# One block for the softmax and the weighing of a graph attention layer, with shares by logarithm and scatters dealt out anew

## The reference

```python
kj = k[src] + e                                  # e = edge_attr @ We
vj = v[src] + e
alpha = jnp.einsum('ehc,ehc->eh', q[dst], kj) / np.sqrt(C)
amax = jax.ops.segment_max(alpha, dst, num_segments=n)
ex = jnp.exp(alpha - amax[dst])
denom = jax.ops.segment_sum(ex, dst, num_segments=n)
alpha = ex / (denom[dst] + 1e-16)                # the share of an edge
agg = jax.ops.segment_sum(vj * alpha[:, :, None], dst, num_segments=n)
out = agg.reshape(n, HID) + (x @ Wskip + bskip)
```

## Time and profile before

| | us |
|---|---|
| median of 3 runs | 5401.89 |
| lowest and highest run | 5398.77, 5412.19 |
| span of the profiled execution, from its first to its last instruction | 4651.0 |
| `softmax_maxima`, from 2061 to 2197 | 136.0 |
| `weigh_values`, from 2197 to 2400.7 | 203.7 |
| m1 and l2, from 2400.7 to 2568.6 | 167.9 |

### The profile page before, as it was taken

How to read it: one execution, slowest core, us unless ns; L and a number is a source line. 1 busy time by engine, 2 the same in 40 slices (tenths; PEclk the granted TensorE clock), 3 DMA queues, 4 the chain that set the end, 5 groups by cost and what they waited for, 6 DMA issues and landing times. The chain is left out here.

```text
span 4651.0 us, 50018 instructions
## 1 busy us (share of the span) xinstructions
PE 2871.3 (62%) x13750; PEld 2210.0 (48%) x13751; DVE 2230.8 (48%) x2711; ACT 613.9 (13%) x1076; POOL 3414.1 (73%) x3213
## 2 busy tenths in 40 slices
PE   3799998967777777751989643444444333333333
PEld 1688887943333333331989433333333333333333
DVE  7899997656666666668971621111111111111112
ACT  0355554010000000001751000000000000000000
POOL 1888886857777777767867677777777777777775
PEclk8899999968877878875999866666666566555556
DMA  6466566816666666651989523222222122212221
GB/s 191 139 189 183 170 187 209 265 37 172 170 170 170 170 171 173 173 153 59 278 241 276 174 68 94 68 68 68 68 68 68 49 53 52 53 53 53 53 53 51
DMA packets 498663, 599.91 MB, mean 129 GB/s; under 512 B 190115, under 2 KB 367441, under 8 KB 496248
## 3 DMA queue, kind: packets, MB, share of 16 engines
q0 software_dynamic: 117856, 246.12, 19.4%
q1 hardware_dynamic: 337751, 229.77, 17.7%
q10 hardware_dynamic: 42944, 122.68, 7.3%
HBM read 406.69 MB, written 204.36 MB: 131 GB/s over the span
## 5 line engine op out<-in xcount | busy, mean ns | idle before, releaser
L1151 PE MATMUL ps<-got,g_hot 128*128 x3224 | 719.2, 414 | 1151.3 <-DMA got<-y_back,s_msg 597.5
L721 POOL DMA_INDIRECT rec_by_src<-rec,pos x782 | 1123.9, 1437 | 344.1 <-issue 245.8
L1151 PEld LDWEIGHTS ps<-got,g_hot 128*128 128x128 f32 x3224 | 667.8, 316 | 1213.1 <-issue 1213.1
L1612 POOL DMA_INDIRECT sc_kv<-kv,d_src x806 | 762.0, 945 | 254.9 <-issue 245.3
L1036 POOL DMA_INDIRECT got<-y_forward,d_msg x782 | 739.1, 945 | 238.2 <-issue 238.2
L1036 POOL DMA_INDIRECT got<-y_back,s_msg x766 | 722.7, 943 | 241.7 <-issue 233.1
L806 PE MATMUL ps<-ln_low,ln_hot 128*125 128x256 f32 x2848 | 618.9, 380 | 19.7 <-DVE ln_low L783 15.9
L806 PEld LDWEIGHTS ps<-ln_low,ln_hot 128*125 128x125 f32 x2848 | 535.3, 188 | 103.2 <-issue 22.7
L1059 DVE TENSOR_TENSOR g_hot<-ps,src_loc 128x1024 f32<-128x1024 f32 x101 | 123.4, 1224 | 832.1 <-PE ps L1151 831.7
L1715 PE MATMUL ps<-q,sc_hotT 128*128 x1616 | 274.2, 322 | 236.4 <-DVE sc_hotT L1657 207.4
L1067 DVE TENSOR_TENSOR g_y<-ps,ms_b 128x384 f32<-128x384 f32 x75 | 41.8, 558 | 732.1 <-PE ps L1164 732.1
(11 more groups left out here) (328 smaller groups left out, 3102.4 us busy)
## 6 DMA issues: line engine op xcount, KB each, us to landing
linked<-ln_out SPq DMA_DIRECT2D x320, 224.0 KB
ve<-sc_kve ACTq DMA_DIRECT2D x202, 256.0 KB
wv_ve<-ve SPq DMA_DIRECT2D x101, 512.0 KB, 5.0
l_links<-linked SPq DMA_DIRECT2D x25, 800.0 KB, 7.3
l_links<-linked ACTq DMA_DIRECT2D x25, 800.0 KB, 9.2
attr_pairs<-ln_feats POOLq DMA_DIRECT2D x7, 2048.0 KB
sc_attr<-attr_pairs SPq DMA_DIRECT2D x202, 64.0 KB, 2.6
sc_kv<-kv,d_src POOLq DMA_INDIRECT x806, 3.0
```

What stands on the lines that cost most here:

```text
L721: pool.indirect_dma_start(out=dram["rec_by_src"], out_offset=bass.IndirectOffsetOnAxis(ap=S["pos"][:, c:c + 1], axis=0), in_=S["rec"][:, c ...
L1151: last = pe.matmul(ps[:, bass.ds(columns[j], width)], hot[:, q, j, :], got[:, bass.ds(slots[j], width)], start=False, stop=True, skip_grou ...
L1612: pool.indirect_dma_start(out=kv[:, q, j, :], out_offset=None, in_=dram["kv"], in_offset=bass.IndirectOffsetOnAxis(ap=S["d_src"][:, c:c + ...
```

## The change

The two blocks become one, `softmax_and_weigh`. The node lists and places are loaded in `scores`, in SP's loop at step 24; the -1 is stored in `index_stage`. ACT's Exp writes to `mx_back` and leaves the scores; after the sums ACT takes the logarithm of each head's sums (with 1e-16 added as bias), DVE subtracts it from the scores, and ACT's Exp gives the shares. SP issues the first six loads of values ahead of the stores of the shares. ACT makes its masks of the first three groups, and DVE its masks of the same groups, before the shares are back. The clearing of PSUM is cut in two, 2048 columns early and 1152 behind the first weighing; the transposes back use three banks from the fifth on. At the start of each round of six groups DVE copies that round's shares (192 columns) into PSUM bank 7 (`hand`), and the multiplication reads them there. ACT's first step writes into `wv_hot` itself, not into a buffer of its own. `RECORD_PARTS` is dealt out anew; in `index_stage` ten records go ahead of the gathers. The diff, cut to its core (of `weigh_values`, whose lines move into the new function, only what changes is shown):

```diff
-RECORD_PARTS = {"index": 6, "link": 302, "l0": 70, "m0": 30, "project": 22, "maxima": 82, "weigh": 100, "m1": 42, "l2": 76, "norm": 0}
+RECORD_PARTS = {"index": 16, "link": 302, "l0": 70, "m0": 38, "project": 22, "maxima": 16, "weigh": 138, "m1": 42, "l2": 86, "norm": 0}
...
+            if send is not None:
+                first, last = part_of(send)
+                send_some(pool, S, dram, first, last - LATER)
             for k, s in enumerate(stairs):
...
-                send_records(pool, S, dram, send)
+                send_some(pool, S, dram, last - LATER, last)
...
+                if n == 4 * WAYS:
+                    for name, a in (("before", dram["node"][0:rows]), ("node", dram["node"][1:1 + rows]), ("after", dram["node"][2:2 + rows]),
+                                    ("place", dram["loc"].rearrange("b e -> (b e)")[0:rows])):
+                        sp.dma_start(S["mx_" + name][:, :], a.rearrange("(p c) -> p c", p=P)).then_inc(S["noded"], 16)
...
-def softmax_maxima(nc, S, dram):
+def softmax_and_weigh(nc, S, dram):
...
+        iota = ps[:, 7 * BANK:7 * BANK + P]
+        share = ps[:, 7 * BANK + P:7 * BANK + P + HEADS * WAYS * GROUP].rearrange("p (a c) -> p a c", a=HEADS)
...
+            pe.wait_ge(cleared, 2)
+
+            def group(i, q):
+                columns = load_columns(nc, S, mybir.EngineType.PE, "dst", 1, start_of(i, q))
+                pe.wait_ge(heated[q], i + 1)
+                pe.wait_ge(faced[q], i + 1)
+                pe.wait_ge(weighed[q], i + 1 + (q == WAYS - 1))
+                for j in range(GROUP):
+                    last = pe.matmul(ps[:, bass.ds(columns[j], D)], hot[:, q, j, :], ve[:, q, j, :],
+                                     start=False, stop=True, skip_group_check=True)
+                last.then_inc(summed[q], 1)
+
+            with pe.Fori(0, WHOLE) as i:
...
             send_records(pool, S, dram, "maxima")
+            send_records(pool, S, dram, "weigh")
...
-                act.activation(score[:, h, :], score[:, h, :], ACT.Exp).then_inc(exped, 1)
+                act.activation(back[:, h, :], score[:, h, :], ACT.Exp).then_inc(exped, 1)
+            for h in range(HEADS):
+                act.wait_ge(tallied, h + 1)
+                act.activation(back[:, h, :], back[:, h, :], ACT.Ln, bias=guard[:, 0:1]).then_inc(logged, 1)
+            for h in range(HEADS):
+                act.wait_ge(weighted, h + 1)
+                act.activation(score[:, h, :], score[:, h, :], ACT.Exp).then_inc(shared, 1)
+
+            def face(n):
+                i, q = divmod(n, WAYS)
+                act.wait_ge(summed[q], i + 1)
+                for j in range(OWN, GROUP):
+                    c = n * GROUP + j
+                    last = act.activation(hot[:, q, j, :], S["col"][:, :], ACT.Abs, bias=S["dst_loc"][:, c:c + 1], scale=-1.0)
+                last.then_inc(apart, 1)
+                act.wait_ge(apart, n + 1)
+                act.activation(hot[:, q, OWN:GROUP, :], hot[:, q, OWN:GROUP, :], ACT.Relu, bias=S["ones"][:, 0:1], scale=-1.0).then_inc(faced[q], 1)
+
+            for n in range(FIRST):
+                face(n)
...
+            for n in range(WAYS):
+                bring(n)
             for h in range(HEADS):
                 sp.wait_ge(shared, h + 1)
...
+            dve.wait_ge(S["noded"], 16 * 4)
...
-                link(dve.tensor_scalar_add(back[:, h, :], back[:, h, :], 1e-16))
-                link(dve.reciprocal(back[:, h, :], back[:, h, :]))
-                dve.tensor_tensor(score[:, h, :], score[:, h, :], back[:, h, :], ALU.mult).then_inc(shared, 1)
-            dve.wait_ge(shared, HEADS)
...
+                dve.engine_nop().then_inc(tallied, 1)
+            for h in range(HEADS):
+                dve.wait_ge(logged, h + 1)
+                dve.tensor_tensor(score[:, h, :], score[:, h, :], back[:, h, :], ALU.subtract).then_inc(weighted, 1)
+            dve.wait_ge(weighted, HEADS)
+            dve.wait_ge(turned, HR)
+            dve.wait_ge(kept, HR)
+            dve.memset(ps[:, 0:TURN_AT * BANK], 0.0).then_inc(cleared, 1)
             dve.tensor_copy(iota[:, :], S["col"][:, :]).then_inc(numbered, 1)
             dve.wait_ge(numbered, 1)
+            dve.sem_inc(weighed[WAYS - 1], 1)
+
+            def hand(i):
+                dve.wait_ge(weighed[WAYS - 1], i + 1)
+                dve.tensor_copy(share, S["alpha"][:, :, bass.ds(start_of(i, 0), WAYS * GROUP)]).then_inc(handed, 1)
+                dve.wait_ge(handed, i + 1)
+
+            def mark(i, q):
                 dve.wait_ge(summed[q], i + 1)
                 dve.tensor_tensor(hot[:, q, 0:OWN, :], iota[:, :].unsqueeze(1).to_broadcast([P, OWN, P]),
                                   S["dst_loc"][:, bass.ds(start_of(i, q), OWN)].unsqueeze(2).to_broadcast([P, OWN, P]), ALU.is_equal).then_inc(heated[q], 1)
+
+            def weigh(i, q):
                 dve.wait_ge(landed[q], (i + 1) * 16)
                 ve4 = ve[:, q].rearrange("p k (a c) -> p k a c", c=HEAD)
+                dve.tensor_tensor(ve4, ve4, share[:, :, q * GROUP:(q + 1) * GROUP].rearrange("p a k -> p k a")
                                   .unsqueeze(3).to_broadcast([P, GROUP, HEADS, HEAD]), ALU.mult).then_inc(weighed[q], 1)
 
+            for q in range(FIRST):
+                mark(0, q)
+            dve.wait_ge(done, HR)
+            hand(0)
+            weigh(0, 0)
+            dve.memset(ps[:, TURN_AT * BANK:BLOCKS * D], 0.0).then_inc(cleared, 1)
+            for q in range(1, WAYS):
+                if q >= FIRST:
+                    mark(0, q)
+                weigh(0, q)
+            with dve.Fori(1, WHOLE) as i:
+                hand(i)
                 for q in range(WAYS):
+                    mark(i, q)
+                    weigh(i, q)
+            hand(WHOLE)
             for q in range(REST):
+                mark(WHOLE, q)
+                weigh(WHOLE, q)
```

More of the change, by code:

```diff
@@ L471, in _ @@
             if send is not None:
-                send_records(pool, S, dram, send)
+                send_some(pool, S, dram, last - LATER, last)
         @block.sync
         def _(sp):
+            sp.wait_ge(fronted, 1)
+            sp.dma_start(dram["node"][0:1].rearrange("(a n) -> a n", a=1), front[:, :]).then_inc(begun, 16)
             for k, s in enumerate(stairs):
@@ L488, in _ @@
             sp.wait_ge(filed, 16 * len(stairs))
+            sp.wait_ge(begun, 16)
             if sent:
@@ L1744, in softmax_maxima @@
         turn = m.sb("mx_turn", [P, HR, P])
-        node = m.sb("mx_node", [P, L])
-        node_b = m.sb("mx_before", [P, L])
-        node_a = m.sb("mx_after", [P, L])
-        loc = m.sb("mx_loc", [P, L])
+        node, node_b, node_a, loc = (S["mx_" + name] for name in ("node", "before", "after", "place"))
         bad = m.sb("mx_bad", [P, L])
@@ L1752, in softmax_maxima @@
         back = m.sb("mx_back", [P, HEADS, L])
-        open_b, open_a, open_s = (m.sb("mx_open" + n, [P, L]) for n in ("before", "after", "same"))
+        open_b, open_a, open_s = node, m.sb("mx_openafter", [P, L]), loc
         ends = m.sb("mx_ends", [P, 2 * HEADS])
@@ L1789, in _ @@
                     pe.wait_ge(refilled[h], 16)
-                if n >= 4:
-                    pe.wait_ge(done, n - 3)
-                pe.transpose(ps[:, (n % 4) * BANK:(n % 4) * BANK + P], turn[:, n, :], S["ident"][:, :]).then_inc(turned, 1)
+                if n >= 3:
+                    pe.wait_ge(done, n - 2)
+                pe.transpose(turned_back(n), turn[:, n, :], S["ident"][:, :]).then_inc(turned, 1)
+            pe.wait_ge(cleared, 2)
[9 more added lines that the diff above has]
+            with pe.Fori(0, WHOLE) as i:
+                for q in range(WAYS):
+                    group(i, q)
+            for q in range(REST):
+                group(WHOLE, q)
         @block.gpsimd
@@ L1809, in _ @@
                 act.wait_ge(turned, HR + n + 1)
-                act.activation(S["alpha"][:, h, c * P:(c + 1) * P], ps[:, (n % 4) * BANK:(n % 4) * BANK + P], ACT.Copy).then_inc(done, 1)
+                act.activation(S["alpha"][:, h, c * P:(c + 1) * P], turned_back(n), ACT.Copy).then_inc(done, 1)
             act.wait_ge(done, HR)
+            for n in range(FIRST, GROUPS):
+                face(n)
+            for q in range(WAYS):
+                act.wait_ge(faced[q], WHOLE + (q < REST))
         @block.sync
         def _(sp):
-            sp.wait_ge(fronted, 1)
-            sp.dma_start(dram["node"][0:1].rearrange("(a n) -> a n", a=1), front[:, :]).then_inc(stored, 16)
-            sp.wait_ge(stored, 16)
-            for t, a in ((node_b, dram["node"][0:P * L]), (node, dram["node"][1:1 + P * L]),
-                         (node_a, dram["node"][2:2 + P * L]), (loc, flat_loc[0:P * L])):
-                sp.dma_start(t[:, :], a.rearrange("(p c) -> p c", p=P)).then_inc(noded, 16)
             for h in range(HEADS):
@@ L1834, in _ @@
                              dram["alpha"][h].rearrange("(c p) e -> p c e", p=P)).then_inc(refilled[h], 16)
```

(30 more changed lines are left out.)

90 lines of the change are left out of this document (31 added, 59 removed).

## The result

The changed kernel takes 5527.55 us (median of 4 runs, 5522.1 to 5537.37), the kernel before 5401.58: a ratio of 1.0224 with a 95% interval of 1.0206 to 1.0243. It is 126 us slower, where I had forecast 18 us less.

The account below looks back on a forecast made before the run. The softmax was taken as a serial chain on DVE, the weighing as bound by PE and DVE level. Terms -6.3 - 21.6 - 3.7 + 6.1 + 7.6 = -17.9 us gave 5384.0 us, range 5366 to 5403.

Parts of the forecast that it names:

- the 750.9 us: Whole kernel: difference between profiled span 4651.0 us and median 5401.89, kept unchanged in the forecast.
- The 154 records of the joint block: Softmax and weighing: 28 fewer records on POOL, which would be done earlier still; no effect on time.
- Start of the softmax: Block start to first work on the scores: early node lists and masks gain 6.3 us, at most 9.4.
- Division: First carry to last share: logarithm, subtraction and Exp replace reciprocal and multiplication, 31.85 to 10.25 us, gaining 21.6.
- Way back: Last share to first product of the weighing: 19.0 us becomes some 15.4, gaining 3.7, between 1 and 5.
- Loop: Weighing rounds: `hand` adds 0.68 us a round, less savings; 6.1 us lost in all, bounds 0 to +25.
- a dear copy: Rival, weighing loop: `hand` costs its upper bound, 1.84 us a round, giving 5402.6, no change; chance 0.10.
- values bound by DMA: Rival, weighing: early start only moves the wait, loop takes back half of 31.6 us, giving 5399.8; chance 0.05.
- the rival that had it twice as long: Rival, weighing: multiplication with repeated PSUM shares takes twice 1.22 us, costing 123 us, giving 5507; chance 0.08.
- The records in l2: Block of m1 and l2: ten more records make POOL end 7.6 us after PE, lengthening the block by 7.6.
- m0: Stage m0: eight more records, 10.2 us, fit in an idle of 15.12 us; no effect.
- `index_stage`: Ten records ahead of the first gather, 12.7 us within POOL's 18.43 us wait: nothing, at most 12.7.

Follow-up runs that it names:

- the run with slower records: Changed kernel with three small POOL clearings ahead of each of the 138 later records, no pause: 5415.03 us, ratio 1.0009 against the kernel before.
- the second profile of the kernel before: The kernel before, unchanged, profiled once more: 5398.07 us, span 5396.3.
- The pause with shares from SBUF: Changed kernel; POOL waits after 60 records for PE's first round, then sends 94; weighing reads shares from SBUF without copies: 5408.33 us, ratio 0.9992.

## Why the prediction was wrong

Two steps failed, and they have one root.

- "I keep the 750.9 us between them as they are." That difference was not a constant outside the stages. It lay in them: 263 us in `scores`, 139 in m1 with l2, 270 in the gathering sums, and so on, in stretches in which POOL issues one indirect transfer after another. A span a seventh below the timed median should have been taken as a sign that the traced execution lacked something that the timed ones have.
- "The 154 records of the joint block: [...] With 28 fewer it is done earlier still: nothing." Earlier is what cost the time. Before, POOL was through with its 82 records when the shares came back, stood still at the end of the block, and was then held to one record in 1.87 us by DVE's multiplications. Now nothing stops it at the way back, DVE has nothing to multiply there, records go out at 1.27, PE crawls, so DVE goes on waiting, so records go on at 1.27: the state keeps itself up until the records are out. (Reading the shares from SBUF doesn't end it, 418.5 us, as there is no multiplication to lengthen a record while DVE waits.) The crawl costs 109.5 us by the run with slower records (423.8 against 314.3); less the 23.4 that the rest of the change gains in this block, that is the 86 us. I had looked at POOL only as an engine that may end a block, not as one that slows another. POOL's pause and its first slow records in the second profile of the kernel before:

```profile
2489.90 0.97 POOL L721 DMA_INDIRECT rec_by_src<-rec,pos  x1 [8.53 <-POOLq L1742]
...
2496.68 1.56 POOL L721 DMA_INDIRECT rec_by_src<-rec,pos  x1 [0.31 <-issue]
2498.55 1.56 POOL L721 DMA_INDIRECT rec_by_src<-rec,pos  x1 [0.30 <-issue]
```

The rest, by the terms, where the crawl is kept away (the run with slower records, block 314.3 us; the forecast's sum gives 337.7 - 25.5 = 312.2):

- Start of the softmax: right. 18.1 us to the scores (18.4 in the changed kernel), forecast 18; 6 us gained.
- Division: right, 9.97 us against 10.25. The logarithm takes 1.07 us for 816 columns with its neighbour's overlap (four in 4.30), four subtractions take 3.78 and four Exp 3.20, a little less than assumed. Exp's table load starts 0.02 us behind the last logarithm and Exp 0.01 behind the load; the pause that the Trainium skill, "ScalarE: Activation LUTs", section "What ACT_TABLE_LOAD costs", adds to a switch of tables doesn't show here either, its 1283 ns does (1.28).
- Way back: too hopeful. From last share to first product it is 18.6 us in that run and not 15.4: 0.4 us gained on the earlier trace rows, not 3.7, and nothing on the second profile of the kernel before, which has 17.9 (2477.93 to 2495.78).
- Loop: right. A round takes 11.89 us where 11.88 were forecast, the copy 0.36; the block with the copies is 5.0 us longer than the one without (314.3 against 309.3), the term was 6.1. So the rivals of a dear copy and of values bound by DMA fall. The multiplication from PSUM takes 1209 ns, which disposes of the rival that had it twice as long:

```profile
L2011 DVE TENSOR_TENSOR wv_ve<-wv_ve,ps 128x1024 f32<-128x1024 f32 x101 | 122.1, 1209 | 8.8 <-DMA wv_ve<-ve 8.7
```

- The records in l2: right that they cost, wrong why. Not POOL's end but the crawl counts there, and each of the ten costs its 1.3 us from the first: 13.2 us, not 7.6. The same in m0, where I had put nothing: some 11 us.
- `index_stage`: right, nothing.

With the terms as measured, block -23.4 by that run (314.3 against 337.7), l2 +13.2 and m0 +11, the sum is +0.8 us: without the crawl in the joint block the change would have come out even. The run with slower records agrees (1.0009). The pause with shares from SBUF, whose block is 5 us shorter without the copies, gives 0.9992.

Open: what PE and a dense row of indirect transfers share. That the pace of the records brings the crawl on is shown by the runs above; how it does so is not. The crawl's waits have no releaser in the profile, and ACT and SP show such pauses too (in l2 of the kernel before ACT stood 96.5 us ahead of a copy whose input had been there for some 80 us); whether it is the fetching of instructions, or the writing of something, the trace's own records included, wasn't tried. Some of it can be narrowed from the trace of the changed kernel: from 2541 to 2611, in the crawl, the queues that carry instructions moved a single packet (8 KB at 2567.76, in 1.55 us), so that a wait for such a packet can't stand ahead of each product; the DMA engines are busy for 0.08 of their time there and for 0.86 in the loop (rows below), so that it isn't their load; and the lower clock adds 0.25 us to a product, not the 1.7 to 3.1 us of waiting ahead of it. Why the first trace of the kernel before is free of the crawl isn't known either: the runs that list a span have it 1.7 to 1.9 us below their time, but that trace has no time of its own. So a dense row of records is not enough by itself in every execution. Nor was it tried whether the gathers of `scores` and of the sums could be spaced with profit.

## What to carry to other kernels

When a profile's span and the timed median differ by more than the ends of the program can hold, take a second profile before using its durations. An engine that is off the path can still slow the one on it: look at what happens to PE's rate in each stretch where POOL issues indirect transfers back to back, and count a transfer there at its full time. Spacing them, with a cheap instruction that takes some 0.4 us, can make the whole faster.

## What the runs showed of the hardware

- While POOL issued indirect scatters of 0.97 us every 1.27 to 1.30 us, PE started 0 to 8 products in nearly every ten microseconds of the timed executions (the joint block of the changed kernel, m1 with l2 of the kernel before); at one in 1.42 us 5 to 11 in most; at 1.65, 1.82 and 1.87 its full 84 to 90. The zeros stand in m1, where PE's next product needs a copy that ACT started 96.5 us late: ACT is held up as well. PE returned to its rate some 10 us after the last record. The first trace of the kernel before, whose span lies so far below the timed runs, has records at 1.27 us in l2 and no crawl.
- In the crawl PE's clock falls as well. Two stretches of the changed kernel, in the crawl and in the loop at full rate, columns as above:

```profile
2550.00:2610.00 60.00, 7.81 (x22) 6.04 (x21) 2.87 (x3) 3.20 (x8) 43.54 (x46) 0.50 0.08 18
2650.00:2800.00 150.00, 144.69 (x1230) 141.96 (x1229) 146.75 (x166) 122.36 (x306) 0.00 (x0) 1.00 0.86 268
```

  The granted clock is 0.50, the lower of its two levels (1.2 GHz), where PE is nearly idle, and 1.00 (2.4 GHz) where it works without gaps; a product takes 0.37 us in the one and 0.12 in the other.
- A multiplication on DVE with both operands in SBUF lengthened the scatter beside it from 0.97 to 1.56 us; with one operand in PSUM it stayed at 0.96.
